# Blocks of the second expert layer: rows turned behind the gate-and-up product, and copied ahead of the gated product

## The reference, cut to what matters

```python
def moe(xn, Wg_s, Wu_s, Wd_s, Wg_r, Wu_r, Wd_r, W_router, routing_bias):
    ...
    scores, idx = jax.lax.top_k(probs, TOPK)            # TOPK = 2 of ER = 7
    ...
    g = jnp.einsum('th,ehi->tei', xt, Wg_r)             # 256 -> 256, each expert
    u = jnp.einsum('th,ehi->tei', xt, Wu_r)
    hmid = silu(g) * u
    combined = jnp.einsum('tei,eih,te->th', hmid, Wd_r, wts)
    return (shared + combined).reshape(B, S, H)
```

## Time and profile before

| what | us |
|---|---|
| runs | 1820.48, 1820.89, 1825.39 |
| median of the runs | 1820.89 |
| span of the profiled execution, first to last instruction | 1819.4 |
| first gate-and-up matmul of block 0, from the span's start | 1026.00 |
| first gate-and-up matmul of block 37 | 1149.18 |

### The profile page before, as it was taken

How to read it: one execution, slowest core, us unless ns; L and a number is a source line. 1 busy time by engine, 2 the same in 40 slices (tenths; PEclk the granted TensorE clock), 3 DMA queues, 4 the chain that set the end, 5 groups by cost and what they waited for, 6 DMA issues and landing times. The chain is left out here.

```text
span 1819.4 us, 33679 instructions
## 1 busy us (share of the span) xinstructions
PE 1573.1 (86%) x11798; PEld 1136.1 (62%) x11830; DVE 983.0 (54%) x2513; ACT 483.2 (27%) x1045; POOL 401.9 (22%) x734
## 2 busy tenths in 40 slices
PE   5878999999968988799979899668888887999992
PEld 3654888889857743355544555445655664798992
DVE  4555344444369957766646333479887456222224
ACT  2331101101066631355522111223331431111010
POOL 0102211111042001111102244333111111344440
PEclk9999999999969999899999999878999999999996
DMA  4104888988721007234315132210000001799995
GB/s 141 38 2 145 302 300 292 308 293 301 231 62 36 2 1 195 82 85 110 82 32 168 33 81 77 70 38 18 1 1 1 1 2 47 260 315 318 314 320 187
DMA packets 162223, 240.64 MB, mean 132 GB/s; under 512 B 19808, under 2 KB 109344, under 8 KB 161984
## 3 DMA queue, kind: packets, MB, share of 16 engines
q1 hardware_dynamic: 149440, 208.35, 35.4%
q0 software_dynamic: 10512, 28.72, 5.8%
q10 hardware_dynamic: 2160, 2.10, 0.3%
HBM read 208.96 MB, written 30.15 MB: 131 GB/s over the span
## 5 line engine op out<-in xcount | busy, mean ns | idle before, releaser
L1543 DVE TENSOR_REDUCE l1a_nm<-l1a_sc 128x1 f32<-128x512 f32 (+3 forms) x256 | 107.1, 482 | 53.7 <-PE l1a_sc L1679 53.7
L2309 PEld LDWEIGHTS e0b_gp<-e0b_xT,e0b_wgu 128*128 128x128 f32 x936 | 107.4, 192 | 14.5 <-issue 12.3
L2309 PE MATMUL e0b_gp<-e0b_xT,e0b_wgu 128*128 128x128 f32 x936 | 114.9, 279 | 1.8 <-DVE e0b_hT L2379 1.3
L2330 PE MATMUL e0b_yp<-e0b_wd,e0b_hT 128*128 128x256 f32 x468 | 115.1, 388 | 0.6 <-issue 0.6
L2360 ACT ACTIVATE e0b_sg<-e0b_gp 128x640 f32<-128x640 f32 x78 | 33.5, 481 | 285.3 <-PE e0b_gp L2309 285.3
L2330 PEld LDWEIGHTS e0b_yp<-e0b_wd,e0b_hT 128*128 128x128 f32 x468 | 82.6, 189 | 21.9 <-issue 13.9
L2309 PE MATMUL e0b_up<-e0b_xT,e0b_wgu 128*128 128x128 f32 x780 | 93.5, 275 | 0.0
L2309 PEld LDWEIGHTS e0b_up<-e0b_xT,e0b_wgu 128*128 128x128 f32 x780 | 90.2, 192 | 0.0
L2309 PE MATMUL e3b_gp<-e3b_xT,e3b_wgu 128*128 128x128 f32 x624 | 78.1, 278 | 5.9 <-DMA e3b_wgu<-in_L_ffn_W 4.8
L2309 PEld LDWEIGHTS e3b_gp<-e3b_xT,e3b_wgu 128*128 128x128 f32 x624 | 73.9, 192 | 14.7 <-DMA e3b_wgu<-in_L_ffn_W 7.3
L2464 PE MATMUL e1b_gu<-e_kgu,e1b_xT 128*128 x152 | 75.2, 617 | 4.4 <-DVE e1b_xT L2529 2.8
(11 more groups left out here) (606 smaller groups left out, 3536.3 us busy)
## 6 DMA issues: line engine op xcount, KB each, us to landing
e3b_wgu<-in_L_ffn_W SPq DMA_DIRECT2D x78, 512.0 KB, 5.3
e0b_wgu<-in_L_ffn_gate_proj SPq DMA_DIRECT2D x39, 704.0 KB, 4.4
e0b_wgu<-in_L_ffn_up_proj SPq DMA_DIRECT2D x39, 704.0 KB, 5.8
e0b_wd<-in_L_ffn_down_proj SPq DMA_DIRECT2D x39, 640.0 KB, 5.2
e3b_wd<-in_L_ffn_W SPq DMA_DIRECT2D x39, 512.0 KB, 6.9
x_rows<-xn SPq DMA_DIRECT2D x3, 2048.0 KB, 8.6
l_parts<-l1p_split SPq DMA_DIRECT2D x16, 384.0 KB, 3.1
l_stack_k<-l_parts SPq DMA_DIRECT2D x48, 128.0 KB, 2.8
```

The source lines that it names most:

```text
L1543: nc.vector.tensor_reduce(nm[:, g % 2, q, i:i + 1], sc[q], AX_X, ALU.max, negate=True).then_inc(max_done, 1)
L2309: last = nc.tensor.matmul(dst[:, f, :], wgu[j][:, k, at + f * P:at + (f + 1) * P], xT[j][:, k, :], start=(k == 0), stop=(k == KC - 1))
L2330: last = nc.tensor.matmul(yp[:], hT[j][0:FW[f], f, :], wd[j][0:FW[f], f, :], start=(f == 0), stop=(f == FC - 1))
```

## The change

In `kept_blocks`, TensorE now does the row transposes of block n + 1 directly behind the gate-and-up product of block n, ahead of the hidden transposes of block n - 1. VectorE does the row copy of block n + 1 ahead of the gated product of block n. Every instruction is kept; two orders change.

```diff
                         gate_up(n, own[n])
                         if n + 1 < NB:
                             own.append(expert(n + 1))
+                            turn_rows(n + 1)
                         if n >= 1:
                             turn_hidden(n - 1)
-                        if n + 1 < NB:
-                            turn_rows(n + 1)
                         if n >= 2:
                             down(n - 2, own[n - 2])
                     turn_hidden(NB - 1)
...
                     copy_rows(0)
                     for n in range(NB):
-                        hidden(n)
                         if n + 1 < NB:
                             copy_rows(n + 1)
+                        hidden(n)
                         if n >= 2:
                             copy_out(n - 2)
                     copy_out(NB - 2)
```

## The result

| | before | changed |
|---|---|---|
| median of the runs, us | 1820.89 (4 runs) | 1806.01 (4 runs) |
| all runs, us | 1820.48 to 1825.39 | 1801.86 to 1809.78 |
| span of the profiled execution, us | 1819.4 | 1804.9 |
| ratio | | 0.991, 95% interval 0.9887 to 0.9933 |

The change makes the kernel 0.9% faster. 1809.0 was predicted, with a range from 1805 to 1814. The median lies in the range, but the ratio puts the time at 0.991 x 1820.89 = 1804.5, half a us under its lower end. With the two later timings in which the same pair ran, the means are 1821.6 us (62 runs of the kernel before) and 1806.8 (16 of the changed one): 14.8 us, with a standard error of 0.9, against 11.9 forecast. So the question of the experiments is not whether it works but where some 3 us beyond the sum come from.

What follows compares the result with a forecast made beforehand. The prediction took the loop through silu, `h` and row copy, for which TensorE waits, as the block stage's bound. 2 x 0.53 + 35 x 0.31 = 11.9 us off the span gave 1807.5, plus 1.5 for the median: 1809.0, range 1805 to 1814.

Steps and rivals of the forecast that it cites:

- 0.31 us of each turn is a hole: Block stage: TensorE idles 0.31 us before each gate product, in all 37 periods of 3.33; the change removes it.
- the floor of 3.02: Block stage: with the copy early, TensorE's own work sets the new period, 3.02 us instead of 3.33.
- First turns: Between blocks 0 and 1, and 1 and 2: the copy chain bounds, 2.79 to 2.80 instead of 3.33, 0.53 saved each.
- The loop: Block stage: gate product, silu, `h`, row copy, gate product sets the period of 3.33 us, and TensorE waits for it.
- Copy start 2.24: Block stage, VectorE: the row copy starts 2.24 us behind the gate start, no longer waiting for the silu.
- Slack 0.22: Block stage: the gate load at 2.79 is some 0.22 us ahead of the point where it costs anything.
- Rival A: Block stage: gate weight load stays exposed or copy is 0.2 late; period 3.13, gain 8.1, time 1812.8; chance 0.09.
- Rival B: Block stage: waits for gathered rows put the hole back; only the first turns gain, time 1820; chance 0.08.
- the stages behind: Lookup stage after the blocks: only its phase against the clock moves, a few us both ways; 3 us either side.
- D: Stages behind the blocks: the clock goes the favourable way, 3 to 5 us more gain than forecast, 1805; chance 0.05.
- C: Stages behind the blocks: lookup stage meets a lower clock, 17.6 us lost, 1826.6, slower than before; chance 0.04.
- no row shows the phase: Lookup stage: no profile row shows where its work falls in the free-running count that sets the slow clock phase.

Runs made afterwards that it cites:

- 5 matmuls: Kernel before, plus 5 TensorE matmuls whose result nobody reads, in front of the last down product: ratio to before 0.9991 (0.9979 to 1.0003).
- 9 matmuls: Changed kernel, plus 9 TensorE matmuls whose result nobody reads, in front of the last down product: ratio to before 0.9945 (0.9927 to 0.9962).
- copy twice: Changed kernel with VectorE doing each row copy two times, first to a tile nobody reads: ratio to before 0.9969 (0.9947 to 0.9992).

## Why the prediction was right, and where it was wrong

**The bound and its size: right.** "0.31 us of each turn is a hole" and the floor of 3.02: measured 3.33 and 3.02. First turns 2.80 as forecast, blocks 0 to 37 in 111.27 against 111.3, block stage 11.9 us shorter against 11.9. The loop was the one named: taking `h` out of the front of the copy removes it, and TensorE's order alone gains nothing.

**The parts.** Copy start 2.24 behind the gate start: 1041.81 - 1039.67 + 0.10 = 2.24. Start of `h` 2.58, and gate load 2.91 where about 2.9 was forecast, by the same sum. Slack 0.22: confirmed by the doubled copy. Rival A, the load not pulled under the down product, did not happen even with the load at its edge (VectorE alone). Rival B: no wait for gathered rows; landing at most 4.0. What the prediction did not say is that one half of the change would have done nearly all of it.

**The step that failed: the stages behind, taken as zero in the sum with 3 us of clock to either side, 0.05 for more gain (D) and 0.04 for a loss (C), and "no row shows the phase".** Half of the phase could be read: the granted clock around 1159 in the trace of before has the fall 1.8 us behind the stage's start. What another place would give, no row of before could say, and so the sum had nothing for the term that the runs then measured at 1.8, 5.4 and 1.9 us in the three profiles of the changed kernel, 3.0 in the mean, always as a gain: 11.9 + 3.0 = 14.9 against the 14.8 of the timings. Seen afterwards, the old place is a bad one. It gives 223.8 to 223.9 in all six profiles of either order with that fall, and only one of the eighteen profiles, with the fall at +2.6, is slower (224.8), so the bounds to either side should not have been alike. C had the right place and the wrong sign. That the median of the first four runs, 1806.0, lies inside the range is due to the width for the clock, not to the mechanism that was forecast.

**Open.** Why the same fall gives 222 in some executions and 218.5 in another is half answered: the clock's low stretch that starts at +34.1 ends at +47.7 in one and at +51.1 in the others, but why it does isn't known. What keeps VectorE idle for 2.1 us in the kernel before with 5 matmuls isn't known either. The part of the clock in the 3 us is shown by the same instructions at both levels, by where VectorE's instructions part in the traces, and by two kernels of the new order (9 matmuls, copy twice) that lose the gain when the fall comes at +1.6 to +1.7. That it is all of the 3 us in the timings is a sum from three profiles, with a standard error of 0.9 on the timings.

## What to carry to other kernels

Read a nearly full TensorE by the distance of starts and by the idle time of its weight loads, not by busy time: 98.5% busy hid 9% of the stage. On an in-order engine that serves two loops, put the instruction for which the bound engine waits ahead of the one whose reader comes a turn later, even if its input is ready later. And when a stage gets shorter, look where the stage behind it falls against the clock: compare whole-kernel gains with the stage's own, and don't credit the difference to the edit.

## What the runs showed of the hardware

The distance from the start of the block stage to the fall of the clock behind it repeats to 0.1 us between executions of one kernel (138.1 to 138.2; 124.5), although the stage itself starts up to 6.6 us apart. The Trainium skill ("TensorE: Matmul & The Clock Gate", Part 1) says that the place of a clock transition varies from run to run, because the count behind it runs free. Measured from the start of the execution that is so here (the fall comes at 1144.2, 1150.6 and 1150.8 in the three profiles of the changed kernel), but the stage moves with it, so against the stage the place is fixed.

A weight load on TensorE that is released 0.11 us behind the start of the last matmul ahead of it cost nothing (VectorE's order alone: load at 1061.20, last down matmul at 1060.44 + 3 x 0.217 = 1061.09, period 3.02). In copy twice the load could go 3.13 behind the gate start, 0.23 behind the last down matmul by the sums of the prediction, and the turn was 0.11 longer.

Single executions scatter by 17 us in the kernel before and by 12 in the changed one (1813.47 to 1830.38 and 1801.86 to 1813.72), up to 6.7 of it ahead of the block stage.
